# Who makes the low halves of the expert weights, and where the first chunk's rows lie: one Trainium2 core, a mixture of experts around an attention-like layer

## Chip, cores, metric

The kernel runs on one core of a Trainium2 chip. The metric is the device time of one execution in microseconds (us), median of the runs; lower is better. Engines: PE is TensorE's matmul, PEld its weight load, DVE is VectorE, ACT is ScalarE, POOL is GpSimd, SP is SyncE, which issues most DMAs.

## The reference, cut to what matters

```python
x = x + 0.5 * ffn(layernorm(x), ...)      # T = 2048 rows of D = 512
x = x + attn(layernorm(x), ...)           # 6 heads, a rotating recurrence over the rows
x = x + 0.5 * ffn(layernorm(x), ...)      # the same weights again

def ffn(x):                               # E = 8 experts, top 2, hidden 352
    scores = xf @ gate_w.T + gate_b + bias
    top_scores, top_idx = top_k(scores, 2)
    gates = softmax(top_scores)
    h = silu(einsum('td,ehd->teh', xf, w1) + b1)
    y = einsum('teh,edh->ted', h, w2) + b2
    out = einsum('ted,te->td', y, comb)   # comb: the gates at the chosen experts
```

## The kernel before, in words

Matrix products run in float16 with operands in two halves: a high half (the value times 256 for weights, rounded to float16) and a low half (what the rounding left). Three products (high by high, high by low, low by high) stand for one product of float32.

**Three phases.** The first mixture of experts (phase 0), the attention layer in four chunks of 512 rows, the second mixture (phase 1). A mixture first routes: `route` on VectorE and TensorE turns the scores into 39 slot tiles (`SLOT_TILES`) of 128 rows, each belonging to one expert, in the order of the experts. Its matmuls on TensorE are `route` (lines 647 to 654) and `slot_gates` (656 to 660). Then `slots` works tile by tile. GpSimd gathers a tile's 128 rows (line 537). TensorE transposes them (`xt`, through line 609), multiplies by w1 (`up`, 12 matmuls through line 615), transposes the hidden rows (`ht`, line 687) and multiplies by w2 (`down`, 9 matmuls through line 615). ScalarE makes the high half of the rows (`x_high`, line 972), the SiLU (line 977) and the high half of the hidden rows (`h_high`, line 982). VectorE makes the low halves (`x_low`, line 1361, and `h_low`, line 1372), adds the bias (line 1367) and scales the output (`y_out`, line 1380), which GpSimd scatters to `y_rows` (line 541). Each engine has its own list of instructions; a step's order is written out by hand: on TensorE `ht(t)`, `up(t+1)`, `xt(t+2)`, `down(t)`, on ScalarE `h_high(t)`, `silu(t+1)`, `x_high(t+2)`, on VectorE `h_low(t)`, `add_bias(t+1)`, `x_low(t+2)`, `y_out(t)`. The first 8 tiles (2 x `PEELED`) are written out, the rest is a hardware loop.

**The experts' weights.** In phase 0 the weights come as float32 (2944 values per partition and expert, `FW`) through three staging buffers `wstage`. VectorE makes both halves of experts 0 and 1 ahead of the routing (`split_low`, lines 1256 and 1259). For experts 2 to 7 ScalarE makes the high half (`split_high`, line 941) and VectorE the low half (`split_low`, line 1259): for expert 2 before the first `add_bias`, for experts 3 to 7 after the steps of tiles 0 to 4. SP loads expert e into buffer e mod 3 when the low half of expert e-3 is made (semaphore `w_ready`, line 354). When all are made, SP stores them to `w_saved` for phase 1 and fetches the attention weights in pieces, one per two tiles of the loop.

**The start of the attention.** SP waits until the outputs of the last tile are made (line 403, `m_yo`), loads the 512 rows of chunk 0 from `x_in` into the buffer `xgrp` (`group_in`, line 407), waits until the last scatter has landed (line 379), and then loads both contributions per tile of rows from `y_rows` into `y_first`, in eight DMAs (line 433). VectorE adds them (`first_rows`, lines 1452 and 1453), then takes the statistics of the four tiles (line 1250) and the moments. SP stores the rows (`group_out`), and loads chunk 1 into the same buffer (`next_group_in`) when they are stored and normalised; its contributions are added by GpSimd's DMAs (line 547).

The lines that the change touches, beside these: 371 (SP waits for all low halves), 530 (constants), 678 (`up` waits for its expert's weights), 996 to 1002 and 1229 to 1231 on ScalarE, 1401 to 1410 on VectorE.

## Time and profile before

| | |
|---|---|
| median of 3 runs | 895.51 us (894.84 to 895.96) |
| the profiled execution | 895.87 us |
| its span, first to last instruction | 894.1 us |
| busy PE, PEld | 737.8 us (83%), 406.8 us (45%) |
| busy DVE, ACT, POOL | 622.1 us (70%), 348.1 us (39%), 236.3 us (26%) |
| mean granted TensorE clock | 0.922 of 2.4 GHz |
| chain of waits, shares of the span | PE 70%, DVE 15%, DMA 5%, issue 4%, ACT 3% |

The span is what the trace covers. A busy share says how long an engine had an instruction in it, not how fast it went. The chain follows back from the last instruction, at each step to what released it. "issue" in it is time in which the engine waited for nothing that the profile shows. The granted clock is 1.0 at 2.4 GHz and 0.5 at 1.2 GHz.

### The profile page before, as it was taken

The numbers are of one execution on the slowest core, as the hardware profiler recorded it, in microseconds if no ns is written. First come the engines' busy times: TensorE is split into PE (matmuls) and PEld (weight loads), VectorE is DVE, ScalarE is ACT, GpSimd is POOL, SyncE is SP. The second block draws the span as 40 slices with busy tenths as digits, with TensorE's granted clock in tenths as the row PEclk, the third lists the DMA queues.
The fourth block names the chain that finished last, engine by engine and source line by source line (L and its number), as shares of the span: only waits on it lengthen the run. The fifth ranks groups of instructions, "written<-read, shape, count | busy, mean of one in ns | idle before, by whom it ended". The sixth has DMA issues, their size and how long they took to land.

```text
span 894.1 us, 13749 instructions
## 1 busy us (share of the span) xinstructions
PE 737.8 (83%) x4128; PEld 406.8 (45%) x4129; DVE 622.1 (70%) x1009; ACT 348.1 (39%) x600; POOL 236.3 (26%) x222
## 2 busy tenths in 40 slices
PE   8527699999990898997999999999529999999910
PEld 5215455555550444443444444444316565656600
DVE  6886755566654269999989998995775555555545
ACT  5714333434320546445644654532703323333300
POOL 3115644444520101101211011021113434444300
PEclk9859999999995899899999999999859999999965
DMA  9936568865425430610441201363836733333269
GB/s 321 385 111 207 186 223 317 322 243 176 143 83 199 99 89 21 121 49 0 88 78 24 60 12 25 120 166 128 311 112 223 255 107 117 117 106 117 84 223 374
DMA packets 45305, 137.25 MB, mean 153 GB/s; under 512 B 5840, under 2 KB 5840, under 8 KB 41936
## 3 DMA queue, kind: packets, MB, share of 16 engines
q1 hardware_dynamic: 27888, 86.38, 26.8%
q0 software_dynamic: 17376, 50.34, 20.5%
q8 instruction: 23, 0.38, 0.2%
q14 instruction: 18, 0.15, 0.0%
HBM read 85.32 MB, written 51.38 MB: 153 GB/s over the span
## 4 chain that ended last, share of the span: by engine, by line
PE 70%; DVE 15%; DMA 5%; issue 4%; ACT 3%; SPq 1%; POOL 0%; DVEq 0%; POOLq 0%; ACTq 0%
PE bank L615 59%; PE bank L609 4%; PE bank L687 3%; DMA space<-y_rows 2%; PE bank L804 2%; DVE space L1469 1%; DVE space L1466 1%; DVE space L1259 1%; DVE bst L1250 1%; SPq L477 1%; DMA y_rows<-space,slot_dst 1%; DVE space L1316 1%; DMA space<-x_in 1%; DMA space<-xn_rows,slot_src 1%; PE bank L738 1%
## 5 line engine op out<-in xcount | busy, mean ns | idle before, releaser
L615 PE MATMUL bank<-space 128*128 (+3 forms) x2958 | 581.0, 349 | 44.5 <-DVE space L1320 25.6
L615 PEld LDWEIGHTS bank<-space 128*128 128x128 f16 (+1 forms) x2958 | 274.3, 99 | 296.2 <-issue 37.7
L541 POOL DMA_INDIRECT y_rows<-space,slot_dst x78 | 99.7, 1278 | 158.2 <-DVE space L1380 158.2
L1361 DVE TENSOR_TENSOR space<-bank,space 128x512 f16<-128x512 f32 x78 | 54.0, 692 | 84.8 <-issue 43.2
L537 POOL DMA_INDIRECT space<-xn_rows,slot_src x78 | 76.3, 978 | 130.4 <-PE bank L609 70.0
L977 ACT ACTIVATE space<-space 128x352 f32<-128x352 f32 x78 | 38.7, 496 | 177.3 <-DVE space L1367 174.8
L1367 DVE SCALAR_TENSOR_TENSOR space<-bank,space 128x352 f32<-128x352 f32 x78 | 40.9, 524 | 64.0 <-PE bank L615 49.1
L609 PE MATMUL bank<-ident,space 128*128 128x128 f32 x440 | 67.6, 284 | 12.4 <-DMA space<-xn_rows,slot_src 10.5
L982 ACT ACTIVATE space<-bank 128x384 f16<-128x384 f32 x78 | 38.3, 491 | 77.9 <-PE bank L687 76.7
L1380 DVE TENSOR_SCALAR space<-bank,slot_gate 128x512 f32<-128x512 f32 x78 | 58.5, 750 | 12.9 <-PE bank L615 10.3
L1466 DVE SCALAR_TENSOR_TENSOR space<-space,cang 128x512 f32<-128x512 f32 x84 | 63.0, 750 | 5.5 <-ACT space L1051 3.3
L609 PEld LDWEIGHTS bank<-ident,space 128*128 128x128 f32 x440 | 55.1, 147 | 21.3 <-issue 14.1
L565 POOL TENSOR_TENSOR space<-space,power 128x8 f32<-128x8 f32 x12 | 23.8, 1986 | 137.4 <-ACT space L1079 137.4
L972 ACT ACTIVATE space<-bank 128x512 f16<-128x512 f32 x78 | 45.2, 580 | 26.8 <-PE bank L609 26.8
L1051 ACT ACTIVATE space<-bank 128x512 f32<-128x512 f32 x48 | 28.6, 595 | 60.0 <-PE bank L615 59.5
L1372 DVE TENSOR_TENSOR space<-bank,space 128x384 f16<-128x384 f32 x78 | 43.2, 554 | 10.0 <-ACT space L982 6.7
L1469 DVE SCALAR_TENSOR_TENSOR space<-space,conv_sb 128x512 f32<-128x512 f32 x72 | 48.7, 747 | 0.0
L687 PE MATMUL bank<-ident,space 128*128 128x128 f32 x234 | 40.4, 282 | 7.3 <-issue 7.0
L687 PEld LDWEIGHTS bank<-ident,space 128*128 128x128 f32 x234 | 27.0, 141 | 31.8 <-issue 25.0
L738 PE MATMUL bank<-ident,space 128*128 128x128 f32 x64 | 12.7, 344 | 32.8 <-ACT space L1020 30.5
L575 POOL DMA_DIRECT2D x_rows<-space x12 | 10.6, 882 | 101.2 <-ACT space L1100 101.2
L615 PE MATMUL bank<-space,gw 128*8 128x256 f32 x128 | 31.0, 386 | 0.6 <-ACT space L964 0.6
(172 smaller groups left out, 697.4 us busy)
## 6 DMA issues: line engine op xcount, KB each, us to landing
space<-ffn_w SPq DMA_DIRECT2D x8, 1472.0 KB, 10.0
w_saved<-space SPq DMA_DIRECT2D x8, 1472.0 KB
space<-w_saved SPq DMA_DIRECT2D x8, 1472.0 KB, 9.5
space<-y_rows SPq DMA_DIRECT2D x40, 256.0 KB, 6.0
xn_rows<-space SPq DMA_DIRECT2D x8, 1024.0 KB, 6.1
space<-x_in SPq DMA_DIRECT2D x7, 1024.0 KB, 5.3
space<-att_w SPq DMA_DIRECT2D x12, 518.0 KB
space<-y_rows POOLq DMA_DIRECT2D x6, 1024.0 KB, 9.3
```

Of the source, the lines that this page charges most:

```text
L537: gp.indirect_dma_start(dst, None, rows, bass.IndirectOffsetOnAxis(ap=index, axis=0)).then_inc(done, 16)
L541: gp.indirect_dma_start(y_rows, bass.IndirectOffsetOnAxis(ap=slot_dst[:, t:t + 1], axis=0), yo[:, t % 2], None).then_inc(y_st[t % 2], 16)
L609: last = pe.transpose(dst[:, k * P:(k + 1) * P], src[:, k * P:(k + 1) * P], ident[:, :])
L615: last = pe.matmul(dst, a, b, start=(n == 0), stop=(n == len(terms) - 1))
L687: last = pe.transpose(bank[4 + par][:, c * P:(c + 1) * P], hact[:, par, c * P:(c + 1) * P], ident[:, :])
L972: act.activation(xh[:, par], bank[par][:, :], ACT.Copy).then_inc(m_xh, 1)
L1361: v.tensor_tensor(xl[:, par], bank[par][:, :], xh[:, par], ALU.subtract).then_inc(m_xl, 1)
L1367: v.scalar_tensor_tensor(z[:, par], bank[2 + par][:, 0:HID], UNSCALE, b1_bc[:, bass.ds(ev * HID, HID)], ALU.mult, ALU.add).then_inc(m_zb, 1)
L1372: v.tensor_tensor(hl[:, par].rearrange("p a b -> p (a b)"), bank[4 + par][:, 0:KH * P], hh[:, par].rearrange("p a b -> p (a b)"), ALU.subt ...
L1380: v.tensor_scalar(yo[:, par], bank[6 + par][:, :], UNSCALE / GSCALE, slot_gate[:, bass.ds(t, 1)], ALU.mult, ALU.mult).then_inc(m_yo, 1)
L1466: seq(v.scalar_tensor_tensor(a, raw[:, p, kind, j:j + CH], cang[:, p, kind, j:j + 1], a, ALU.mult, ALU.add))
L1469: return ch(v.scalar_tensor_tensor(vcon[:, par, eo], raw[:, p, 2 + eo, j:j + CH], conv_sb[:, p, 2 + eo, j:j + 1], vcon[:, par, eo], ALU.mu ...
```

## The change

For experts 2, 3 and 4 the low half is no longer made by VectorE. TensorE multiplies the staged float32 weights by the identity, takes the high half times 1/256 away in the same bank of PSUM (a float16 product with a diagonal of -1/256, `unscale`), and ScalarE copies the difference times 256 to the low half. This goes in pieces of up to 512 columns (`CUTS`, six per expert), through four banks for experts 2 and 3 and two for expert 4. On TensorE the twelve pieces of experts 2 and 3 stand between the two counting products of `route` and the product over the one-hot rows; four pieces of expert 4 stand ahead of `xt(0)` and two behind it. On ScalarE the high half of expert 4 stands behind the twelve pieces of experts 2 and 3. VectorE keeps experts 5, 6, 7, after the steps of tiles 1, 2, 3; ScalarE's high halves of these come after tiles 0, 1, 2. SP waits for the new semaphore `w_low` for the buffers of experts 2 to 4. In the 8 written-out tiles of phase 0, ScalarE makes `x_high(t+2)` ahead of `silu(t+1)`.

Chunk 0's rows get a buffer of their own, so SP no longer waits for the last tile's outputs before it loads them, and chunk 1's rows are loaded right behind the `y_first` loads. These are four DMAs in place of eight. VectorE takes each tile's statistics right behind its sums. ScalarE's first write to the second `oh` buffer waits until chunk 0 is stored.

```diff
+BYPE = 3
+CUTS = [(at, min(CH, FW - at)) for at in range(0, FW, CH)]
+LOW_BANKS = (6, 7, 0, 1)
...
+        group_rows = [Layout(first_at)([TPC, D])] + [xgrp] * (NCH - 1)
...
             def weights_in(e):
-                if e >= STAGES:
+                if OWN <= e - STAGES < OWN + BYPE:
+                    sp.wait_ge(w_low, len(CUTS) * (e - STAGES - OWN + 1))
+                elif e >= STAGES:
                     sp.wait_ge(w_ready, e - STAGES + 1)
...
                 sp.wait_ge(s_slotg, 1)
-                sp.wait_ge(w_ready, E)
+                sp.wait_ge(w_ready, E - BYPE)
+                sp.wait_ge(w_low, len(CUTS) * BYPE)
...
             slot_weights()
-            sp.wait_ge(m_yo, SLOT_TILES + 2)
...
             def next_group_in(c):
-                sp.wait_ge(x1_st, 16 * c)
-                sp.wait_ge(c_xn, TPC * c)
+                if c > 1:
+                    sp.wait_ge(x1_st, 16 * c)
+                    sp.wait_ge(c_xn, TPC * c)
                 group_in(c)
...
             for i in range(TPC):
-                for k in (0, 1):
-                    sp.dma_start(y_first[:, k, i], y_rows[bass.ds(k * T + i * P, P), :]).then_inc(yf_in[i], 16)
+                sp.dma_start(y_first[:, :, i], y_rows[0:2 * T, :].rearrange("(k n p) d -> n p k d", k=2, p=P)[i]).then_inc(yf_in[i], 16)
+            next_group_in(1)
             group_out(0)
-            next_group_in(1)
...
+            def low_piece(e, i):
+
+                n = len(CUTS) * (e - OWN) + i
+                at, w = CUTS[i]
+                b = LOW_BANKS[n % 4] if e < OWN + BYPE - 1 else LOW_BANKS[n % 2]
+                pe.wait_ge(w_hi, e - OWN + 1)
+                if n >= 4:
+                    pe.wait_ge(w_low, n - (3 if e < OWN + BYPE - 1 else 1))
+                pe.matmul(bank[b][:, 0:w], ident[:, :], wstage[:, e % STAGES, at:at + w], start=True, stop=False, skip_group_check=True)
+                pe.matmul(bank[b][:, 0:w], unscale[:, :], wexp[:, e, at:at + w], start=False, stop=True,
+                          skip_group_check=True).then_inc(w_diff, 1)
...
                 products(bank[4][:, 0:NT * E], [(ones[:, :], chosen)]).then_inc(s_count, 1)
+                if not ph:
+                    pe.wait_ge(consts, 3)
+                    for e in range(OWN, OWN + BYPE - 1):
+                        for i in range(len(CUTS)):
+                            low_piece(e, i)
                 pe.wait_ge(s_ohs, ph + 1)
...
+                if not ph:
+                    for i in range(4):
+                        low_piece(OWN + BYPE - 1, i)
                 pe.wait_ge(s_route, ph + 1)
                 xt(0, 0, 0)
+                if not ph:
+                    for i in range(4, len(CUTS)):
+                        low_piece(OWN + BYPE - 1, i)
                 pe.wait_ge(m_xl, o + 2)
...
+            def low_piece(e, i):
...
+                act.wait_ge(w_diff, n + 1)
+                act.activation(wexp[:, e, FW + at:FW + at + w], bank[b][:, 0:w], ACT.Copy, scale=WSCALE).then_inc(w_low, 1)
...
+                def first_step(t, par):
+                    h_high(t, par)
+                    x_high(t + 2, par)
+                    silu(t + 1, 1 - par)
...
-                    step(t, t % 2)
-                    if not ph and 1 <= t <= 3:
-                        split_high(t + 4)
+                    if ph:
+                        step(t, t % 2)
+                    else:
+                        first_step(t, t % 2)
+                    if not ph and t < E - OWN - BYPE:
+                        split_high(OWN + BYPE + t)
...
-            for e in range(OWN + 1, 5):
-                split_high(e)
+            split_high(OWN + 1)
+            for e in (OWN, OWN + 1):
+                for i in range(len(CUTS)):
+                    low_piece(e, i)
+            split_high(OWN + 2)
+            for i in range(4):
+                low_piece(OWN + 2, i)
...
                 x_low(0, 0)
-                if not ph:
-                    split_low(OWN)
                 add_bias(0, 0)
...
-                    if not ph and OWN + 1 + t < E:
-                        split_low(OWN + 1 + t)
+                    if not ph and 1 <= t <= 3:
+                        split_low(OWN + BYPE + t - 1)
...
                 for i in range(TPC):
-                    v.wait_ge(yf_in[i], 32)
-                    seq(v.tensor_tensor(xgrp[:, i], xgrp[:, i], y_first[:, 0, i], ALU.add))
-                    v.tensor_tensor(xgrp[:, i], xgrp[:, i], y_first[:, 1, i], ALU.add).then_inc(c_sum, 1)
+                    v.wait_ge(yf_in[i], 16)
+                    seq(v.tensor_tensor(group_rows[0][:, i], group_rows[0][:, i], y_first[:, 0, i], ALU.add))
+                    v.tensor_tensor(group_rows[0][:, i], group_rows[0][:, i], y_first[:, 1, i], ALU.add).then_inc(c_sum, 1)
                     v.wait_ge(c_sum, i + 1)
+                    ch(v.bn_stats(bst[:, i], group_rows[0][:, i]))
+                ch.wait()
...
                 first_rows()
-                variance(xgrp)
+                moments()
```

## Rows read from the trace of the kernel before

**Rows 1.** Chain of waits, routing and tiles 0 to 5 (start us, us, what).

```profile
57.15 3.48 DMA space<-xn_rows,slot_src
...
80.36 2.13 PE bank L615 x9
```

**Rows 2.** Timeline of PE, 20 to 72 us (start us, us, operation).

```profile
28.47 1.89 PE L615 MATMUL bank<-space,gw 128*8 128x256 f32 x8
...
40.74 0.63 PE L615 MATMUL bank<-space,ones 128*128 128x128 f32 x2
54.16 1.25 PE L615 MATMUL bank<-space 128*128 128x39 f16 x32 [12.78 <-DVE space L1320]
60.76 1.09 PE L609 MATMUL bank<-ident,space 128*128 128x128 f32 x4 [5.36 <-DMA space<-xn_rows,slot_src]
63.57 3.70 PE L615 MATMUL bank<-space 128*128 x12 [1.72 <-DVE space L1361]
...
71.11 0.55 PE L687 MATMUL bank<-ident,space 128*128 128x128 f32 x3 [0.97 <-issue]
```

**Rows 3.** Timeline of PE in chunk 0 of the attention.

```profile
315.80 9.45 PE L615 MATMUL bank<-space 128*128 128x512 f16 x43
```

**Rows 4.** Timeline of ACT, routing and tiles 0 and 1.

```profile
39.15 2.64 ACT L941 ACTIVATE space<-space 128x2944 f16<-128x2944 f32 x1
...
74.56 0.58 ACT L972 ACTIVATE space<-bank 128x512 f16<-128x512 f32 x1
76.19 0.49 ACT L982 ACTIVATE space<-bank 128x384 f16<-128x384 f32 x1 [1.05 <-PE bank L687]
```

**Rows 5.** Stretches: us, busy PE, PEld, DVE, ACT, POOL, PEclk, DMA share, GB/s.

```profile
42.00:60.00 18.00, 1.25 (x32) 1.13 (x32) 16.71 (x43) 2.66 (x1) 2.16 (x2) 0.50 0.45 173
69.00:70.00 1.00, 1.00 (x38) 0.93 (x35) 0.69 (x1) 0.00 (x0) 0.34 (x1) 0.94 0.96 400
296.00:298.00 2.00, 0.96 (x4) 0.29 (x4) 0.00 (x0) 1.84 (x4) 0.00 (x0) 0.95 0.83 313
301.00:301.50 0.50, 0.50 (x4) 0.13 (x2) 0.00 (x0) 0.00 (x0) 0.38 (x1) 0.78 0.00 0
```

**Rows 6.** Timeline of DVE, tiles 0 to 7.

```profile
72.29 0.56 DVE L1372 TENSOR_TENSOR space<-bank,space 128x384 f16<-128x384 f32 x1 [1.91 <-ACT space L982]
...
76.53 3.22 DVE L1259 SCALAR_TENSOR_TENSOR space<-space 128x2944 f16<-128x2944 f32 x1
79.67 0.55 DVE L1372 TENSOR_TENSOR space<-bank,space 128x384 f16<-128x384 f32 x1
...
99.61 0.55 DVE L1372 TENSOR_TENSOR space<-bank,space 128x384 f16<-128x384 f32 x1
...
106.27 0.55 DVE L1372 TENSOR_TENSOR space<-bank,space 128x384 f16<-128x384 f32 x1
...
111.24 0.56 DVE L1372 TENSOR_TENSOR space<-bank,space 128x384 f16<-128x384 f32 x1 [1.38 <-ACT space L982]
...
115.98 0.55 DVE L1372 TENSOR_TENSOR space<-bank,space 128x384 f16<-128x384 f32 x1
```

**Rows 7.** Chain of waits, the last scatter of each phase and the rows behind.

```profile
268.53 6.27 DMA y_rows<-space,slot_dst
...
285.07 2.48 DVE bst L1250 x4
...
855.62 2.73 DMA y_rows<-space,slot_dst
```

**Rows 8.** Timeline of DVE, the first rows of the attention.

```profile
278.22 0.69 DVE L1452 TENSOR_TENSOR space<-space 128x512 f32<-128x512 f32 x1 [2.98 <-DMA space<-y_rows]
...
280.71 0.69 DVE L1452 TENSOR_TENSOR space<-space 128x512 f32<-128x512 f32 x1 [1.08 <-DMA space<-y_rows]
```

**Rows 9.** Timeline of SP, end of phase 0.

```profile
268.28 0.40 SPq L407 DMA_DIRECT2D space<-x_in  x1
274.82 3.68 SPq L433 DMA_DIRECT2D space<-y_rows  x8
```

More of the change, by code:

```diff
@@ L113, in build @@
         minus = sb("minus", [P, P], F16)
+        unscale = sb("unscale", [P, P], F16)
         sel = sb("sel", [44, 2, PAIRS, P], F16)
@@ L250, in build @@
         on = lay([2, CH])
+        first_at = lay.at
         oh.append(lay([2 * PAIRS, CH], F16))
@@ L283, in build @@
         w_ready = sem("w_ready")
+        w_diff = sem("w_diff")
+        w_low = sem("w_low")
         w_save = sem("w_save")
@@ L402, in _ @@
             slot_weights()
-            sp.wait_ge(m_yo, SLOT_TILES + 2)
             def group_in(c):
-                sp.dma_start(xgrp, rows4(x_in, c)).then_inc(cg_in, 16)
+                sp.dma_start(group_rows[c], rows4(x_in, c)).then_inc(cg_in, 16)
             def group_out(c):
@@ L413, in group_out @@
                     sp.wait_ge(cy_in[1], 16 * c)
-                sp.dma_start(rows4(x_rows, c), xgrp).then_inc(x1_st, 16)
+                sp.dma_start(rows4(x_rows, c), group_rows[c]).then_inc(x1_st, 16)
             def next_group_in(c):
-                sp.wait_ge(x1_st, 16 * c)
-                sp.wait_ge(c_xn, TPC * c)
+                if c > 1:
+                    sp.wait_ge(x1_st, 16 * c)
+                    sp.wait_ge(c_xn, TPC * c)
                 group_in(c)
@@ L530, in more_constants @@
                     select(sel_rows, sel_rows, ALU.not_equal, 1.0, -first, [[-1, NAB], [0, 64]], 1)
+                seq(gp.memset(unscale[:, :], 0.0))
+                seq(gp.affine_select(out=unscale[:, :], in_=unscale[:, :], compare_op=ALU.not_equal, fill=-UNSCALE, base=0,
+                                     pattern=[[-1, P]], channel_multiplier=1))
                 seq(gp.memset(minus[:, :], 0.0))
@@ L676, in up @@
                             pe.wait_ge(w_back[t], 16)
+                        elif OWN <= t < OWN + BYPE:
+                            pe.wait_ge(w_low, len(CUTS) * (t - OWN + 1))
                         else:
-                            pe.wait_ge(w_ready, t + 1)
+                            pe.wait_ge(w_ready, t + 1 if t < OWN else t + 1 - BYPE)
                     pe.wait_ge(m_xl, o + t + 3)
@@ L941, in split_high @@
                 act.activation(wexp[:, e, 0:FW], wstage[:, e % STAGES], ACT.Copy, scale=WSCALE).then_inc(w_hi, 1)
+            def low_piece(e, i):
+                n = len(CUTS) * (e - OWN) + i
+                at, w = CUTS[i]
+                b = LOW_BANKS[n % 4] if e < OWN + BYPE - 1 else LOW_BANKS[n % 2]
+                act.wait_ge(w_diff, n + 1)
+                act.activation(wexp[:, e, FW + at:FW + at + w], bank[b][:, 0:w], ACT.Copy, scale=WSCALE).then_inc(w_low, 1)
             def normalise_row(ph, n):
@@ L991, in step @@
                     x_high(t + 2, par)
+                def first_step(t, par):
+                    h_high(t, par)
+                    x_high(t + 2, par)
+                    silu(t + 1, 1 - par)
                 x_high(0, 0)
+                if not ph:
+                    for i in range(4, len(CUTS)):
+                        low_piece(OWN + BYPE - 1, i)
                 silu(0, 0)
@@ L996, in slots @@
                 for t in range(2 * PEELED):
-                    step(t, t % 2)
-                    if not ph and 1 <= t <= 3:
-                        split_high(t + 4)
+                    if ph:
[4 more added lines that the diff above has]
+                        split_high(OWN + BYPE + t)
                 split = PEELED if ph else PEELED + PIECES
                 if not ph:
-                    act.wait_ge(w_ready, E)
+                    act.wait_ge(w_ready, E - BYPE)
+                    act.wait_ge(w_low, len(CUTS) * BYPE)
                     with act.Fori(PEELED, split) as j:
@@ L1019, in normalise @@
                     act.wait_ge(c_xt, TPC * c + i - 1)
-                act.activation(xnt[:, i % 2], xgrp[:, i], ACT.Identity, scale=rstd[:, 0, 0, i:i + 1],
+                act.activation(xnt[:, i % 2], group_rows[c][:, i], ACT.Identity, scale=rstd[:, 0, 0, i:i + 1],
                                bias=rstd[:, 0, 1, i:i + 1]).then_inc(c_xn, 1)
@@ L1092, in gate_high @@
                     act.wait_ge(c_out, TPC * (c - 1))
+                if u == PAIRS:
+                    act.wait_ge(x1_st, 16)
                 act.activation(oh[c % 2][:, 2 * p:2 * p + 2], on, ACT.Copy).then_inc(c_oh, 1)
```

## The prediction

> **What bounds the kernel now.** I read the page's slices first, then the chain of waits, then the timelines of the two stretches that the diff touches, then SP's queue. The chain lies on TensorE for 70% of the span, but not where the change is. From 42 to 60 us, while VectorE turns scores into slots, TensorE is busy 1.25 us of 18, at the granted clock 0.50 (1.2 GHz), and VectorE 16.71 [rows 5]. In the first tiles VectorE decides: one low half takes 3.22 us, and `h_low` of the next tile starts only behind it [rows 6]. `h_low` starts at 72.29 for tile 0 and 79.67 for tile 1 (7.38 apart), at 99.61 for tile 4 and 106.27 for tile 5 (6.66), at 111.24 and 115.98 for tiles 6 and 7 (4.74, no split between) [rows 6]. The third place is the change of phase: the last scatter of phase 0 takes 6.27 us from issue to landing, that of phase 1 takes 2.73 [rows 7]. SP issues the load of chunk 0 at 268.28 and the scatter starts at 268.53 [rows 7, 9].
>
> The profiled execution took 895.87 us, its span is 894.1, so 1.77 lie around it; the median of the runs is 895.51, 0.36 below it. I work out the change of the span and take it from the median. About 0.2% (1.8 us) is what a measurement of this kernel can tell from no change.
>
> **Price of a piece.** On TensorE a piece is a float32 product of 512 columns and a float16 product of 512. Four float32 products of 256 columns took 1.89 us at full clock [rows 2], so one of 512 costs 2 x 0.47 = 0.945. 43 float16 products of 512 took 9.45 [rows 3], 0.22 each. A piece is 1.16 us at 2.4 GHz and twice that, 2.3, at 1.2 GHz. That has not run here in this mixture, so the bounds are 0.58, since ScalarE empties a bank of 512 in that time [rows 4], and 2.3. I take 1.16, because both terms come from the same kinds of product. The sixth piece has 384 columns, so six count as 5.75. ScalarE's 0.58 per piece hides behind TensorE's.
>
> **Routing.** The pieces of experts 2 and 3 begin when the counting products end, 41.4 [rows 2]. Expert 3's high half is ready at 41.8 [rows 4], in time. The clock is at 0.50. It rose about 5.5 us after dense matmuls began at 63.57 (0.94 in the mean from 69 to 70), and 3.4 us after a fall at 297.8 (the stretch from 296 has 0.95, so 0.2 us at half; that from 301.0 has 0.78, so it rose at 301.2) [rows 2, 5]. I take a rise at 45.2: 3.8 us at half give 1.65 pieces, the other 9.85 (twelve count 11.5) take 11.4 us, end 56.6. The one-hot product that started at 54.16 is 2.4 us late; it took 1.25 at half clock [rows 2], some 0.7 now, so it ends 57.3 and not 55.4. That is on the path: the first gather's index comes 1.9 us late. The gather took 3.48 us to land [rows 1], so it lands about 62.6.
>
> ScalarE empties the last piece at 57.2, makes expert 4's high half (2.64 [rows 4]) until 59.9, and TensorE makes four pieces until 64.6 (4 x 1.16). Only then comes `xt(0)`, which started at 60.76 [rows 2]; the gather is in by then, so its lateness is covered. `xt(0)` 0.55 at full clock, two pieces 2.03, `up(0)` from 67.2, 1.8 in place of 3.70 at half clock [rows 2], `xt(1)` 0.45, the 64 gate products 1.7 (38 of them took 1.00 [rows 5]), the 0.97 idle ahead of `ht(0)` as before: `ht(0)` at 72.1 and not at 71.11 [rows 2]. **Cost +1.0.** Expert 2's low half of 3.22 us that VectorE loses ahead of the first `add_bias` gave nothing: TensorE was in `up(0)` until 67.27.
>
> **The first tiles.** Between tiles 0 and 1 VectorE has no split any more, 4.74 in place of 7.38. But ScalarE now makes expert 5's high half behind `silu(1)`: 2.64 us from about 75.1 on the old scale, so `h_high(1)`, which started at 76.19 [rows 4], starts near 77.75, 1.5 late, and nothing hides that. The step takes 6.0 to 6.2: **-1.4**, bounded by 0 (the high half takes all of it) and -2.64. The steps of tiles 1, 2, 3 keep their split. Moving `x_high` ahead of the SiLU I cost at nothing: in a split step `y_out` waits for `down`, which starts 0.14 behind the end of `h_low` and takes 2.13 [rows 1], so an earlier `x_low` only waits longer; elsewhere `down` covers the SiLU that comes 0.6 later. Tile 4 loses its split: 6.66 becomes 4.7, **-1.95**. The buffers of experts 5, 6, 7 come free earlier than before, so no load is late. The longer list of constants on GpSimd lies in an idle stretch before the first gather; if that cover were gone it would be under 1 us.
>
> **Start of the attention.** Chunk 0's load no longer runs beside the last scatter. I take the landing of phase 1's last scatter, 2.73 in place of 6.27: **-3.54**, bounded by 0. By the Trainium skill ("DMA: Bandwidth & Descriptors", Queues, rings and completion order) each DMA engine goes round-robin between the queues that have work, a packet at a time. By this rule the scatter would lose to the load only about its own transfer time, some 1 us, and the sum below would come to 891.0. The trace shows 3.54 between the two landings, and I follow it. Of the `y_first` loads, eight issues took 3.68 us [rows 9]; tile 0 now needs one of four and not two of eight, **-0.4**. VectorE began tile 0 at 278.22 and idled 1.08 before tile 1 [rows 8]; its statistics, 0.62 of the 2.48 [rows 7], now fill that hole, **-0.7**. Bounds for both together: 0, if chunk 1's load behind them slows the last tiles, and -2.5. The moves on SP and GpSimd for chunk 1 only fill an earlier buffer; VectorE is busy with chunk 0 long after. If that cover were gone, chunk 1 would only be ready earlier.
>
> **Sum.** +1.0 - 1.4 - 1.95 - 3.54 - 0.4 - 0.7 = -7.0; 895.5 - 7.0 = 888.5 us.
>
> **Rivals.**
> - *The clock falls once more.* TensorE idles from 57.3 to 59.9. At 297.8 it fell though TensorE had been busy 0.96 us of the 2 around it [rows 5]. Against it: the gap is one of 2.6 us between stretches of dense matmuls, where that stretch was thin throughout. If it falls, expert 4's pieces start at 2.3 each for some 3.4 us (half that is lost, 1.7) and the rest shifts, up to `up(0)` at its old 3.70: +3, 891.5. Chance 0.2.
> - *The scatter is not slow because of the load.* Sharing by turns costs it only about 1 us; the other 2.5 stay: 891.0. That is the time the skill's rule gives. For it: the late landing may be the writes' own. Against it: the same instruction with nothing beside it took 2.73 [rows 7]. Chance 0.12.
> - *The first gather collides.* Expert 6's load is issued when expert 3's low half is done, about 57.3, right ahead of the gather. If that costs what it cost the scatter, 3.54, the rows land at 66.1, 1.5 behind the pieces: 890.0. Chance 0.1.
> - *Slower.* TensorE stays at 1.2 GHz through the pieces. Its place is between `s_count` and `s_ohs`: 41.4 + 11.5 x 2.3 = 67.9, 11.3 late; expert 4's six add 6.7 more, `up(0)` 1.9: +20, 908. It outweighs the gain as soon as the pieces lose 7 us more than planned, at 1.8 us each for the 11.5. For it: 0.50 through this whole stretch [rows 5]; pairs of float32 loads may not hide either (a counting product of 128 columns took 0.63 at half clock [rows 2], four times that is 2.5 for a float32 product alone). Against it: nothing makes TensorE wait between pieces, and such stretches raised the clock. Chance 0.06.
> - *It does not do what it says:* ScalarE's high half eats the whole of the step between tiles 0 and 1, and the statistics move nothing: 890.5 to 891. Inside the range.
>
> **How the numbers follow.** The forecast has 0.45, the rivals 0.2, 0.12, 0.1, 0.06, the rest 0.07 (half of it better than forecast: a rise of the clock at once and both holes filled give about 886). All but the slower one and a heap of several end below 893.7, so faster 0.87, same 0.06, slower 0.07. The range runs from 885.5 to 893: below, the bounds of the small terms together (-2.5 for 1.1 and no loss in the routing would be -9.4); above, the clock's second fall with a gather that collides.
>
> **What would show it.** Right: low pieces of about 1.16 us on TensorE between 42 and 57, the clock at 1.00 by 47, `xt(0)` near 64.6; `h_low` of tile 1 near 79.3 and of tile 5 near 103.9; a last scatter of under 3.5 us; the statistics in four single rows between the sums; the second tile's sums of the attention about 6.5 us earlier than 280.71 and the span 887. Wrong: pieces of 2 us or more, a wait of VectorE for `s_inv` over 5 us, a last scatter that still takes 6 us with no load beside it, or a chain that shows DMA waits where chunk 1 loads.

## The result, and the profile after

The changed kernel takes 888.14 us (median of 6 runs, 885.63 to 891.24), the kernel before 895.81 in the same set (6 runs, 894.84 to 896.36). The ratio is 0.992, 95% interval 0.9901 to 0.9939: faster by 0.6 to 1.0%. The forecast was 888.5. Two later sets of the same changed kernel gave 3.9 and 6.4 us less than before; all 24 runs have a median of 889.57, and the mean of the three differences is 6.0 us (5.4 when each set counts by its number of runs), not 7.7. The profiled execution took 889.80 us, span 888.0.

The page of the changed kernel, part 1 (busy us, share of the span, instructions) and the slices of the granted clock (tenths of 2.4 GHz):

```profile
PE 756.9 (85%) x4182; PEld 414.6 (47%) x4183; DVE 612.3 (69%) x1006; ACT 358.5 (40%) x618; POOL 232.0 (26%) x224
...
PEclk9899999999995998998999999999759999999975
```

TensorE has 19 us more work and VectorE 10 less, as three low halves of 3.2 us changed hands. The mean clock rose from 0.922 to 0.934.

**The routing.** Timeline of PE in the changed kernel (start us, us, operation):

```profile
39.82 0.77 PE L627 MATMUL bank<-space,before 128*128 128x128 f32 x2 [6.55 <-DVE space L1357]
...
42.94 1.46 PE L667 MATMUL bank<-space,ident 128*128 128x512 f32 x2
...
45.53 1.02 PE L667 MATMUL bank<-space,ident 128*128 128x512 f32 x2
46.38 0.38 PE L668 MATMUL bank<-space,unscale 128*128 128x512 f16 x1
46.60 1.02 PE L667 MATMUL bank<-space,ident 128*128 128x512 f32 x2
...
54.66 0.97 PE L627 MATMUL bank<-space 128*128 128x39 f16 x32
57.95 2.07 PE L667 MATMUL bank<-space,ident 128*128 128x512 f32 x2 [2.32 <-ACT space L978]
...
63.78 0.60 PE L621 MATMUL bank<-ident,space 128*128 128x128 f32 x4
```

A piece takes 1.07 us (45.53 to 46.60). The twelve pieces end at 54.7, and the first 3 us of them ran at a granted clock of 0.50. The one-hot product starts at 54.66 (54.16 before [rows 2]). Then TensorE waits 2.32 us for ScalarE's high half of expert 4, and the first piece behind it takes 2.07 us for its float32 product where 1.02 is usual: the clock was down again. Stretches of the changed kernel (us, busy PE, PEld, DVE, ACT, POOL, PEclk, DMA share, GB/s):

```profile
57.00:58.00 1.00, 0.05 (x1) 0.05 (x1) 0.86 (x7) 0.90 (x1) 0.62 (x1) 0.73 0.91 318
58.00:61.00 3.00, 3.00 (x5) 1.27 (x6) 2.97 (x5) 0.52 (x1) 1.53 (x2) 0.52 0.97 405
```

**The first tiles.** For the steps the start of `y_out` is the better scale than that of `h_low`, since `y_out` waits for `down`, the last thing that TensorE does in a step. Timeline of DVE, changed kernel, tiles 0, 1, 2, 4 and 5 (L1443 is `y_out`, L1322 the split):

```profile
76.36 0.75 DVE L1443 TENSOR_SCALAR space<-bank,slot_gate 128x512 f32<-128x512 f32 x1 [0.63 <-PE bank L627]
...
81.21 0.75 DVE L1443 TENSOR_SCALAR space<-bank,slot_gate 128x512 f32<-128x512 f32 x1 [0.90 <-PE bank L627]
81.87 3.21 DVE L1322 SCALAR_TENSOR_TENSOR space<-space 128x2944 f16<-128x2944 f32 x1
...
87.86 0.75 DVE L1443 TENSOR_SCALAR space<-bank,slot_gate 128x512 f32<-128x512 f32 x1 [1.28 <-PE bank L627]
...
101.17 0.75 DVE L1443 TENSOR_SCALAR space<-bank,slot_gate 128x512 f32<-128x512 f32 x1 [1.28 <-PE bank L627]
...
105.71 0.75 DVE L1443 TENSOR_SCALAR space<-bank,slot_gate 128x512 f32<-128x512 f32 x1 [0.68 <-PE bank L627]
```

The same rows of the kernel before:

```profile
75.86 0.75 DVE L1380 TENSOR_SCALAR space<-bank,slot_gate 128x512 f32<-128x512 f32 x1
...
82.51 0.75 DVE L1380 TENSOR_SCALAR space<-bank,slot_gate 128x512 f32<-128x512 f32 x1
...
102.47 0.75 DVE L1380 TENSOR_SCALAR space<-bank,slot_gate 128x512 f32<-128x512 f32 x1
...
109.11 0.75 DVE L1380 TENSOR_SCALAR space<-bank,slot_gate 128x512 f32<-128x512 f32 x1
```

Tile 0 is 0.50 later than before. Both profiles count from their own first instruction; counted from the counting products (39.82, and 40.18 before) it is 36.54 us against 35.68, 0.86 later. The profile of attention_only, whose code up to there is that of the kernel before, has 34.39, so this figure moves by over 1 us between profiles of the same code. The lengths of the steps do not (6.64 to 6.66 in both). Between tiles 0 and 1 are 4.85 us (6.65 before), between 4 and 5 4.54 (6.64). A step that keeps its split takes 6.65 in both. At tile 8 the changed kernel is 3.9 us ahead (120.81 against 124.69), at the last output 3.6 (263.93 against 267.50).

**The start of the attention.** Chain of waits of the changed kernel:

```profile
264.96 2.72 DMA y_rows<-space,slot_dst
267.69 0.02 issue
267.70 3.54 DMA space<-y_rows
...
271.37 0.70 DVE space L1513
272.09 0.70 DVE space L1514
272.79 0.02 issue
272.82 0.69 DVE bst L1516
273.51 0.60 DVE space L1513
```

The last scatter lands in 2.72 us (6.27 before [rows 7]). Sums and statistics run without a hole from 271.37 to 279.64, 8.27 us; before they took 9.32 from 278.22 [rows 8] to 287.54. So the statistics end 7.9 us earlier. From there 1.8 us are given back: 6.1 is the difference of the spans. The first 0.75 go in the transposes ahead of the dense products, which begin 11.1 us after the statistics (290.74 - 279.64), and 10.35 before. The dense products then win 0.5 back. Timeline of PE, changed kernel:

```profile
290.74 16.90 PE L627 MATMUL bank<-space 128*12 128x512 f16 x72 [0.69 <-ACT space L1086]
```

and the kernel before:

```profile
297.89 17.44 PE L615 MATMUL bank<-space 128*12 128x512 f16 x72 [0.69 <-ACT space L1030]
```

The lead is 7.7 us at their end and still 7.72 where the second chunk's dense products begin. In them it falls to 6.3. Chain of waits of the changed kernel, and its stretch (columns as above):

```profile
418.64 5.96 PE bank L627 x18
```

```profile
418.00:423.00 5.00, 5.00 (x15) 2.07 (x15) 4.86 (x8) 2.31 (x3) 0.00 (x0) 0.53 0.61 189
```

The same of the kernel before:

```profile
426.36 4.53 PE bank L615 x18
```

```profile
421.00:426.00 5.00, 2.96 (x12) 2.19 (x13) 4.90 (x8) 4.48 (x8) 0.00 (x0) 0.50 0.00 0
426.00:431.00 5.00, 5.00 (x22) 2.13 (x20) 4.86 (x7) 2.12 (x4) 0.00 (x0) 0.85 0.62 205
```

Eighteen matmuls take 1.43 us more. Both kernels have the clock down here, but in the changed one the half clock lies over the dense products, and in the one before mostly ahead of them (0.50 in 421 to 426), where TensorE is busy 2.96 of 5 us and the chain of waits lies mostly on ScalarE. In the second mixture, whose first `up` takes 3.70 us in place of 3.30, the lead sinks to 5.65 (`up(1)`: 668.72 against 674.37), and 0.45 of it comes back by the end. So what is given back is, for the most part, where the clock stands in this run. From the second chunk on the profile of attention_only keeps its lead of 6.1 to the end of the attention, and fill_only its 7.1. In the first chunk both win 1.6 us more (72 products in 15.81 us in place of 17.44): their clock stood at 1.00 there, and in the kernel before at 0.50 from 297.8 to 301.2.

### The profile page after: what moved, and what is told of

The parts are those of the page before. It is cut to its first block, busy times and chain, and to the rows that moved or that the text cites. A ratio compares the mean times of both kernels' runs of the same rounds, so it can differ in the third digit from the quotient of the medians.

```text
span 888.0 us, 13883 instructions
## 1 busy us (share of the span) xinstructions
PE 756.9 (85%) x4182; PEld 414.6 (47%) x4183; DVE 612.3 (69%) x1006; ACT 358.5 (40%) x618; POOL 232.0 (26%) x224
## 4 chain that ended last, share of the span: by engine, by line
PE 72%; DVE 15%; DMA 4%; issue 4%; ACT 3%; SPq 1%; POOL 0%; DVEq 0%; POOLq 0%; ACTq 0%
PE bank L627 58%; PE bank L621 4%; PE bank L718 3%; DMA space<-y_rows 2%; PE bank L667 2%; DVE space L1529 2%; PE bank L841 2%; DVE space L1532 1%; DVE space L1322 1%; DVE bst L1313 1%; DMA space<-x_in 1%; PE bank L775 1%; DMA y_rows<-space,slot_dst 1%; DVE space L1710 1%; DVE space L1709 1%
## 5 line engine op out<-in xcount | busy, mean ns | idle before, releaser
L553 POOL DMA_INDIRECT y_rows<-space,slot_dst x78 | 94.0, 1205 | 159.0 <-DVE space L1443 159.0
L1443 DVE TENSOR_SCALAR space<-bank,slot_gate 128x512 f32<-128x512 f32 x78 | 58.5, 750 | 19.4 <-PE bank L627 17.4
```

The source lines that it names most:

```text
L553: gp.indirect_dma_start(y_rows, bass.IndirectOffsetOnAxis(ap=slot_dst[:, t:t + 1], axis=0), yo[:, t % 2], None).then_inc(y_st[t % 2], 16)
L1443: v.tensor_scalar(yo[:, par], bank[6 + par][:, :], UNSCALE / GSCALE, slot_gate[:, bass.ds(t, 1)], ALU.mult, ALU.mult).then_inc(m_yo, 1)
```

## The experiments

Each run is compared with runs of the kernel before on the same chip. Their medians were 894.68 (35 runs; the first four experiments), 895.33 (17; the next four) and 893.55 (24; the last four). Single runs of one kernel spread over 3 to 8 us, so the small questions are decided in the timelines, by the length of a stage. Where a difference in us and a ratio do not quite agree: the first is that of the medians, the second weighs all runs.

**attention_only.** The kernel before with the buffer `group_rows`, SP's order, four `y_first` DMAs and the statistics between the sums.

```diff
-            sp.wait_ge(m_yo, SLOT_TILES + 2)
...
+        group_rows = [Layout(first_at)([TPC, D])] + [xgrp] * (NCH - 1)
...
-                variance(xgrp)
+                moments()
```

> The kernel before with the second half of the change alone: chunk 0's rows in their own buffer and loaded early, chunk 1's load ahead, four y_first DMAs, statistics between the sums. My theory: -3.5 us from the last scatter, -1.1 from the sums and statistics, about -4.6, so 891.2 us, last scatter under 3.5 us. Rival (DMA engines only take turns, the scatter loses about 1 us to the load): -2.1, 893.7 us, last scatter still above 5 us.

Measured: 889.28 us, ratio 0.9953 (0.9935 to 0.997), 5.4 us less than before. The scatter landed in 2.71 us, sums and statistics took 8.28. The ratio makes it 4.2 us; the forecast of 4.6 for this half lies between the two and inside the interval (2.7 to 5.8 us).

**weights_only.** The changed kernel with that half undone.

```diff
+            sp.wait_ge(m_yo, SLOT_TILES + 2)
...
-        group_rows = [Layout(first_at)([TPC, D])] + [xgrp] * (NCH - 1)
...
-                moments()
+                variance(xgrp)
```

> The change with its second half undone: only the low halves of three experts moved and the order on ScalarE in the first eight tiles. My prediction's terms: +1.0 -1.4 -1.95 = -2.35, so 893.4 us. The trace of the changed kernel has the last output of phase 0 3.6 us earlier than before; if that is what the part is worth alone, 892.2 us. Rival (what is won in the first tiles is lost later, so the parts do not add up): 895 us or more.

Measured: 892.65 us, ratio 0.9973 (0.9956 to 0.9991), 2.0 less by the medians and 2.4 by the ratio, near the -2.35 of the prediction. The scatter is back at 5.96 us. The two halves add up to -7.4 by the medians and -6.6 by the ratios, where the whole has -3.9 and -4.8 in the same set (below) and -7.7 and -7.2 in the first. Within this noise nothing shows that they do not add up. In this profile one split step took 8.33 us in place of 6.66, which had not been expected.

**load_late.** The changed kernel, one wait put back.

```diff
             slot_weights()
+            sp.wait_ge(m_yo, SLOT_TILES + 2)
```

> The changed kernel with one wait put back: SP waits for the last tile's outputs before it loads chunk 0's rows, so the 1 MB load again runs beside the last scatter. Collision theory: +3.5 us, scatter about 6.3 us from issue to landing. Turn-taking alone: +1.0 us, scatter 3.7. If the change of the scatter had nothing to do with the load: +0, scatter 2.7.

Chain of waits of this run:

```profile
262.74 5.66 DMA y_rows<-space,slot_dst
268.42 3.46 DMA space<-y_rows
```

The scatter beside the load takes 5.66 us, 2.9 more than in every run without it (2.71 to 2.73 in eleven profiles). For the scatter the collision theory stands; taking turns alone was to cost about 1. The +3.5 us of it are not seen in the time: 891.14 against 890.81 of the changed kernel in the same set, 0.3 us more by the medians and 1.8 by the ratios, with intervals of about 3 us from end to end. In this profile 2.5 us go between the last output and the first sum (10.3 against 7.8), and 2.8 came from elsewhere, as the next run shows.

**changed_again.** The changed kernel unchanged, beside the three above.

> The changed kernel unchanged. Its six runs so far fall into two heaps, 885.6 to 886.5 and 889.8 to 891.2. If the heaps come from when TensorE's granted clock falls and rises, a profile from the lower heap has fewer or shorter stretches at 0.50 than the profiled run at 889.8 (which has 3.4 us at half clock from 57.5 and 30.7 us between the attention and the second mixture). If they do not, the stretches at 0.50 are the same in both and the difference lies in DMA landings.

Measured: 890.81 us (12 runs, 885.6 to 892.59), ratio 0.9946 (0.9928 to 0.9965). No profile of the lower heap came out of it (this one is at 891.68), so the heaps were not compared as planned. The 24 runs of all three sets lie between 885.60 and 892.59 with no gap wider than 1.2 us. But it can be laid beside load_late, whose code up to the last tile is the same. Timeline of PE behind the one-hot product, changed_again:

```profile
58.79 1.94 PE L667 MATMUL bank<-space,ident 128*128 128x512 f32 x2 [2.32 <-ACT space L978]
60.53 0.63 PE L668 MATMUL bank<-space,unscale 128*128 128x512 f16 x1
```

and load_late:

```profile
57.06 1.12 PE L668 MATMUL bank<-space,ident 128*128 128x512 f32 x2 [2.32 <-ACT space L979]
58.02 0.38 PE L669 MATMUL bank<-space,unscale 128*128 128x512 f16 x1
```

The gap is the same, 2.32 us. In changed_again the clock fell at its end (about 59.0, by 0.74 from 58 to 60), in load_late it did not. From the counting products to the first `y_out` it is 36.91 us in changed_again and 34.06 in load_late: 2.85 us. Of these 0.98 lie ahead of the gap, where the clock rose earlier in load_late (its one-hot product starts 14.51 us behind the counting products, 15.49 in changed_again). From the first piece behind the gap to the first `y_out` it is 18.13 against 16.26, so the fall cost 1.9 us. Then changed_again pays once more in a split step, where TensorE waits 1.98 us for VectorE ahead of `down`:

```profile
92.91 3.80 PE L627 MATMUL bank<-space 128*128 x9 [1.98 <-DVE space L1435]
```

```profile
88.00:92.00 4.00, 2.94 (x21) 2.04 (x19) 3.58 (x2) 2.60 (x3) 2.55 (x1) 1.00 0.25 72
92.00:96.00 4.00, 3.09 (x8) 1.26 (x9) 1.80 (x4) 0.50 (x1) 2.13 (x2) 0.64 0.36 123
```

Nine matmuls take 3.80 us, not 2.11, and that step is 8.33 us long.

**warm_gap.** Eleven products that nobody reads fill the gap (added work, the output is the same).

```diff
+                    for i in range(WARM):
+                        pe.matmul(bank[3][:, :], unscale[:, :], wexp[:, 0, 0:CH], start=True, stop=True, skip_group_check=True)
                     for i in range(4):
                         low_piece(OWN + BYPE - 1, i)
```

> The changed kernel with eleven float16 products of 512 columns, whose result nobody reads, between the one-hot product and expert 4's first piece, where TensorE waits 2.3 to 2.6 us for ScalarE's high half. In three of four profiles of kernels with the pieces the granted clock was 0.50 for 3.4 us from about 57, and the first piece began with 2.07 us in place of 1.02. Theory (that fall lengthens the way to the first tile): no stretch at 0.50 there, expert 4's four pieces in 4.3 us, h_low of tile 0 about 1.7 us earlier counted from the counting products, time -1.2 us in the mean, since not every run has the fall. Rival (the fall has nothing to do with the gap, or the gather decides anyway): nothing, or up to +0.5 from the added products.

Measured: 888.56 us, ratio 0.9922 (0.9897 to 0.9947), 6.8 less than before. No clock fall behind the one-hot product. The first `y_out` came 35.39 us after the counting products; the six profiles of kernels with the same order up to there and a fall in the gap have 36.5 to 37.0. A part of this is when the clock first rose. From the first piece behind the gap it is 17.06 us here and 17.96 to 18.51 in the six, so the gap's fall costs 0.9 to 1.45 us more than filling it (load_late, with neither, has 16.26). One profile without a fall does not show that the added products prevent it, since two of the eight with the gap unfilled have none there either. And a split step then took 8.01 us with the clock down, and the time is not told apart from the changed kernel's.

**high5_early.** ScalarE's high half of expert 5 ahead of the first SiLU.

```diff
+                    split_high(OWN + BYPE)
                 silu(0, 0)
...
-                    if not ph and t < E - OWN - BYPE:
+                    if not ph and 1 <= t < E - OWN - BYPE:
```

> The changed kernel with ScalarE's high half of expert 5 moved from behind tile 0's step to behind the last piece of expert 4, ahead of the first SiLU, where ScalarE idles 2.1 us. Prediction's term: between tiles 0 and 1 that high half is exposed, 5.57 us from h_low to h_low where 4.6 would do, so -1.0 us. Rival (the step has other reasons, as the 1.2 us of issue ahead of h_low): the interval stays at 5.5.

Measured: 889.82 us, ratio 0.9926 (0.9898 to 0.9954). From `y_out(0)` to `y_out(1)` 4.50 us in place of 4.85. The exposed part was 0.35 us, not 1.0 to 1.5. Moved ahead of the first SiLU the high half is exposed there: `ht(0)` starts 7.74 us behind `xt(0)`, and 7.11 in load_late, where the clock was up as well. So this profile shows no gain on balance (its clock fell besides in `up(1)`, which took 3.49 us in place of 1.95). The reason for the 0.35 stands in the changed kernel's timelines of ACT and PE, the high half, `h_high(1)` behind it, and `down(1)`:

```profile
75.29 2.65 ACT L978 ACTIVATE space<-space 128x2944 f16<-128x2944 f32 x1
77.84 0.48 ACT L1026 ACTIVATE space<-bank 128x384 f16<-128x384 f32 x1
```

```profile
76.48 1.95 PE L627 MATMUL bank<-space 128*128 x12
78.27 0.60 PE L621 MATMUL bank<-ident,space 128*128 128x128 f32 x4
79.05 2.11 PE L627 MATMUL bank<-space 128*128 x9 [0.18 <-DVE space L1435]
```

`h_high(1)` is late, but what needs it is `down(1)`, and TensorE has `up(2)` and `xt(3)` to do before that. It waited 0.18 us.

**silu_first.** The old order on ScalarE in the first eight tiles.

```diff
                 def first_step(t, par):
                     h_high(t, par)
-                    x_high(t + 2, par)
                     silu(t + 1, 1 - par)
+                    x_high(t + 2, par)
```

> The changed kernel with ScalarE's old order, SiLU ahead of x_high, in the first eight tiles of phase 0. The prediction costed the order at nothing: all intervals of h_low within 0.1 us of the changed kernel's, time the same. Rival: the interval from tile 4 to tile 5 is 3.70 us in the changed kernel's profile and 4.7 was forecast; if the order gives that, it goes back to 4.7 here, +1.0 us.

Measured: 889.55 us, ratio 0.9941 (0.9919 to 0.9963). By `y_out`: the step between tiles 0 and 1 takes 5.25 us in place of 4.85, the three split steps 6.65, 6.65, 6.66 as before, tiles 4 to 5 4.58 (4.54). So the order is worth 0.4 us in one step, where it lets ScalarE's high half start earlier, and nothing in the others. The rival falls: between the `h_low` of tiles 4 and 5 there are 3.71 us here, as in the changed kernel, so the 3.70 was no matter of the order.

**two_experts.** VectorE keeps expert 4 too.

```diff
-BYPE = 3
+BYPE = 2
...
-                    if not ph and t < E - OWN - BYPE:
-                        split_high(OWN + BYPE + t)
+                    if not ph and 1 <= t <= 3:
+                        split_high(t + 4)
...
-                    if not ph and 1 <= t <= 3:
-                        split_low(OWN + BYPE + t - 1)
+                    if not ph and t <= 3:
+                        split_low(OWN + BYPE + t)
```

> The changed kernel with experts 2 and 3 alone made by TensorE and ScalarE; VectorE keeps 4 to 7, behind tiles 0 to 3. Theory (the third expert costs its pieces ahead of xt(0) and saves a split): xt(0) near 60.9 in place of 63.8, at half clock again, h_low of tile 0 about 1.5 us earlier, the interval of tiles 0 to 1 near 7.2 in place of 5.6, so -1.5 + 1.7, the same time within 0.5. Rival (the third expert's pieces are the larger cost): 1.5 us faster.

Measured: 894.72 us, ratio 0.9991 (0.9972 to 1.001). Both theories fall: this is 0.6 us less than before, where the changed kernel had 3.9 to 7.7 less. `xt(0)` started at 61.83, but it waited for the gather, which took 4.89 us to land (3.48 before [rows 1]) beside the weight loads that the pieces had made early. The clock was down for 10.2 us behind the one-hot product, since no pieces fill that stretch. And two of the split steps took 7.2 us, because VectorE now waited for a high half. Timeline of DVE, two_experts:

```profile
92.20 3.23 DVE L1313 SCALAR_TENSOR_TENSOR space<-space 128x2944 f16<-128x2944 f32 x1 [0.48 <-ACT space L974]
```

In the new order ScalarE makes the SiLU behind the wait for `add_bias`, and the high half of the same step only behind that. The changed kernel makes each high half one step ahead and has no such wait. So this run tests two things at once, the number of experts and the later high halves (0.6 us in each of two steps). Its step between tiles 0 and 1 was 8.14 us where 7.2 was expected, with the clock down in `down(1)` (3.61 us for nine matmuls in place of 2.11). How many experts are best with the high halves one step ahead stays open.

**high4_early.** Expert 4's high half ahead of the last four pieces of expert 3.

```diff
                 for i in range(len(CUTS)):
                     low_piece(e, i)
-            split_high(OWN + 2)
+                    if e == OWN + 1 and i == 1:
+                        split_high(OWN + 2)
```

> The changed kernel with ScalarE's high half of expert 4 moved ahead of the last four pieces of expert 3: four banks let TensorE run on meanwhile. TensorE then has no gap behind the one-hot product. Theory (the gap of 2.3 to 3 us, and the fall of the clock behind it, lie on the path to the first tile, the gather does not): expert 4's first piece within 0.3 us of the one-hot product's end, xt(0) at 21 to 22 us after the counting products in place of 24 to 25, the first y_out 2 to 3 us earlier by the same scale, time -2 us. Rival (the first gather decides, which landed 4.9 us from its issue where it was waited for): xt(0) waits for the gather and the gain is under 1.5 us.

Timeline of PE of this run:

```profile
54.00 0.97 PE L627 MATMUL bank<-space 128*128 128x39 f16 x32
54.92 1.10 PE L667 MATMUL bank<-space,ident 128*128 128x512 f32 x2
...
62.11 0.63 PE L621 MATMUL bank<-ident,space 128*128 128x128 f32 x4 [2.65 <-DMA space<-xn_rows,slot_src]
```

The gap behind the one-hot product is gone, as meant, and comes back as a gap of 2.65 us ahead of `xt(0)`. The gather was issued at 56.73 and took 5.25 us. 889.25 us, ratio 0.9935 (0.9912 to 0.9958): the rival was right, a hidden wait took the place of the one removed. The clock fell right behind the new gap (0.50 for 3.4 us from 63.2). The first `y_out` came 36.20 us behind the counting products, 36.54 in the changed kernel.

**fill_only.** Eight products that nobody reads ahead of `down` in the steps of tiles 1 to 3 (added work).

```diff
+                    if not ph and isinstance(t, int) and 1 <= t <= 3:
+                        pe.wait_ge(m_yo, o + t + 1)
+                        for i in range(8):
+                            pe.matmul(bank[6 + par][:, :], unscale[:, :], wexp[:, 0, 0:CH], start=True, stop=True, skip_group_check=True)
                     pe.wait_ge(m_hl, o + t + 3)
```

> The changed kernel with eight float16 products that nobody reads ahead of down in the steps of tiles 1 to 3, where TensorE waits about 2 us for VectorE's split. Four of six profiles with moved low halves show one of these steps at 7.5 to 8.3 us in place of 6.65 and the granted clock at 0.50 for 3.4 us in it. Theory (idle of 2 us in 6.65 lets the clock fall, by chance of where it lies): all these steps at 6.65 and no stretch at 0.50 between 70 and 100 us; time -1 us in the mean. Rival (the fall is not tied to the idle): a step over 7.5 us again.

Measured: 891.14 us, ratio 0.9974 (0.9963 to 0.9985), not better than the changed kernel. The steps of tiles 2 to 4 took 6.65, 6.65, 6.66 with the clock up, and so did those of both_fill (below). Without the added products one split step is longer in six of ten profiles of kernels with moved low halves (7.55 to 8.33), so two without a fall agree with the theory and do not show it. I put the products one tile too early: VectorE's split behind tile 1 holds up `down` of tile 2. In the step of tile 1 they met no wait and stood in the way (timeline of PE):

```profile
78.84 1.89 PE L725 MATMUL bank<-space,unscale 128*128 128x512 f16 x8
80.56 2.11 PE L627 MATMUL bank<-space 128*128 x9
```

That step took 6.23 us in place of 4.85, and the steps between tiles 5 and 8 lost 0.8 more: the whole sequence now lies later against the transfers in the background (DMA share 1.05 from 108 to 112 us), and `y_out(6)` waited for a scatter to land, which it does not in the changed kernel. Timeline of DVE:

```profile
114.39 0.75 DVE L1447 TENSOR_SCALAR space<-bank,slot_gate 128x512 f32<-128x512 f32 x1 [1.68 <-DMA y_rows<-space,slot_dst]
```

**both_fill.** high4_early, high5_early and fill_only together.

```diff
+                    split_high(OWN + BYPE)
                 silu(0, 0)
...
+                        for i in range(8):
+                            pe.matmul(bank[6 + par][:, :], unscale[:, :], wexp[:, 0, 0:CH], start=True, stop=True, skip_group_check=True)
```

> The version that the runs so far point to: expert 4's high half early, expert 5's high half ahead of the first SiLU, and the filling products of fill_only. If the parts add up: -2 -0.4 -1 against the changed kernel, 885 to 887 us. Rival (the first gather holds xt(0), as in two_experts): about -1.5, 888.

Measured: 890.80 us, ratio 0.9965 (0.9948 to 0.9981). The clock stayed up from 45 to 270 us, and it is still no faster than the changed kernel: `xt(0)` waited for the gather again (5.26 us), the products misplaced by a tile cost 1.4, and then the attention began 5.6 us before the clock rose. Its 72 products took 18.50 us, where the profiles range from 15.81 (attention_only, silu_first, fill_only) to that. None of the versions beats the changed kernel beyond its interval.

**changed_third.** The changed kernel unchanged, beside the last three.

> The changed kernel unchanged, on the same chip as the three above, since its medians were 888.1 and 890.8 in two sets. By the clock theory every run draws how many falls it has in the gap behind the one-hot product (1.7 us each) and in the split steps (0.9 to 1.7 us): between 886 and 892, median near 889.5. If the two sets differ by the chip and not by the draw, this one is tight.

Measured: 887.20 us (6 runs, 885.99 to 889.65), ratio 0.9932 (0.991 to 0.9953), 6.4 less than before. It is tighter than the second set (3.7 us over 6 runs, 7.0 over 12) and lower than the median forecast here. Its profile shows a fall in the gap and a split step of 8.33 us, so the draw is there too. That the clock makes most of the spread stands in the runs themselves: over all 24 runs of the changed kernel the mean granted clock goes from 0.930 (891.26 to 892.59 us, four runs) to 0.939 (885.63), the correlation with the time is -0.85, and 0.001 more clock goes with 0.76 us less. Whether the chip has a part in the difference of the sets stays open.

## Why the prediction was right, point by point

- **Price of a piece**, 1.16 us: measured 1.07. The float32 product takes 0.86, not 0.945 as scaled from a row of 256 columns; why that row cost more per column no run shows.
- **Rise of the clock**, forecast at 45.2: 43.8, which is 4.0 us after the counting products began at 39.82. This was one draw: in the twelve profiles with the pieces it is 2.9 to 5.5 us. So the twelve pieces ended at 54.7, not 56.6, and the one-hot product came 0.9 us behind VectorE's last row and not 2.4.
- **Gap and clock behind it.** The forecast had the gap (2.6 us, measured 2.32) and took the clock to stay up; the fall was a rival at 0.2. It happened in the profiled run and in five of the seven other profiles with this gap. Its chance was too low, and its price too high (3 us; 1.9 by changed_again against load_late). The pieces' lower price paid for it: `xt(0)` at 63.78 where 64.6 was forecast, `ht(0)` at 71.61 where 72.1 was. The cost of the routing was +0.5 by these two profiles, not +1.0. That this term came out near is in part luck: counted from the counting products the cost is +0.86, it is over 2 us against the profile of attention_only, and load_late, whose clock rose earlier and did not fall, is 1.6 us faster to the first `y_out` than the kernel before.
- **Tiles 0 to 1**, -1.4 with ScalarE's high half exposed by 1.5: measured -1.80, and exposed is only 0.35 (high5_early). This step of the argument failed. I measured it from `h_low` to `h_low`, and forgot that TensorE works on `up(2)` and `xt(3)` before it needs what is late.
- **The new order on ScalarE**, costed at 0: 0.4 us in one step, nothing in split steps (silu_first).
- **Tile 4**, -1.95: -2.10. Another 0.5 us came in the steps behind it, up to tile 8.
- **The scatter**, -3.54: -3.55 (6.27 to 2.72), and load_late puts 2.9 of it back with one wait. The rule of the Trainium skill ("DMA: Bandwidth & Descriptors", Queues, rings and completion order) that I had set against it tells how the engines share; by it as I applied it the loss is about one transfer time, 1 us, and these runs show three times that.
- **Sums and statistics**, -1.1: -0.79. The single DMA per tile gave nothing: 3.68 us from the scatter's landing to the first sum, 3.42 before. This step of the argument failed too: counting fewer issues ahead of the first sum, as the forecast did for its 0.4, does not tell when the first transfer lands. The statistics in the holes gave 1.05.
- **The first gather collides**, a rival at 0.1: right in itself. It lands in 4.9 to 5.3 us where it is waited for, 1.4 to 1.8 more than before. In the changed kernel the pieces cover it, by an estimate with about 1 us to spare (issued at 57.38, and 5.25 later is 62.6, where `xt(0)` starts at 63.78). Where the clock stays up this is gone: in load_late and high5_early `xt(0)` starts 4.98 and 5.24 us behind the gather's issue. So without the fall the gather would decide next, as in high4_early.
- **Slower, and not doing what it says:** neither; the clock rose 3.0 us after the first piece began.
- **The signs.** `h_low` of tile 1 came at 78.35 (79.3 forecast) and of tile 5 at 102.01 (103.9), the second tile's sums at 273.43, 7.3 us earlier and not 6.5, the span is 888.0 (887). The stages to there did better than forecast, and what lies behind them took it back.

The terms measured give +0.5 -1.8 -2.1 -0.5 -3.55 -0.8 = -8.3, the stages up to the end of the statistics -7.9 (the phase's loop loses 0.3). The forecast of -7.0 came near the profiled pair's -6.1 because the gains in the first tiles were forecast too small, and what comes behind was not in the sum at all: 1.8 us given back in the profiled run, most of it in the second chunk's first products, as the clock stood at half there. The mechanism was right in its main terms (the scatter, the two steps without a split). That 888.5 lies 0.4 us from the 888.14 of the first set is luck: the three sets give 3.9 to 7.7 us.

## What to carry to other kernels

Measure a stage at the point that waits last for it, here `y_out` behind `down`, and ask of anything late what the consumer has to do before it needs it. Work moved onto an idle TensorE can also raise the clock for what follows (`up(0)` took 1.96 us in place of 3.70), but only as long as no gap opens behind it: the fall behind the gap of 2.32 us took back 1.9. A removed gap can reappear at the next late thing, here a gather slowed by loads that the same change had made earlier. A load that nobody awaits yet should be issued before a latency-bound small DMA at the end of a phase, not beside it.

## What the runs showed of the hardware that was not expected

- A small indirect DMA loses more beside a bulk load than the time of its own transfer (an estimate: 0.7 us for 256 KB at the 400 GB/s of [rows 5]): the last scatter (256 KB) takes 2.71 to 2.73 us alone and 5.66 to 6.27 beside 1 MB; the first gather 3.48 alone and 4.89 to 5.26 beside a weight load.
- The same program with the same gap of 2.32 us finds the granted clock at 1.00 in one run and at 0.50 in another. A fall lasted about 3.4 us. In the gap it cost 1.9 us (changed_again against load_late), and a split step of 6.65 became 7.55 to 8.33. The kernel before has the same waits of about 2 us in its five split steps, and neither its profile nor that of attention_only shows a fall in them.
- A float32 product of 512 columns followed by a float16 product of 512 into the same bank takes 0.86 + 0.22 us at a granted clock of 1.00 and 2.1 to 2.3 in all at 0.50, with the next piece right behind.
- While VectorE makes a low half (two operands in SBUF, 3.21 us), GpSimd's issue of a scatter takes 3.7 us in place of 1.0; the kernel before has the same beside its splits (3.72 to 3.74). This is the timeline of POOL in the changed kernel, without and with a split beside it:

```profile
77.39 1.01 POOL L553 DMA_INDIRECT y_rows<-space,slot_dst  x1 [1.80 <-DVE space L1443]
...
82.24 3.71 POOL L553 DMA_INDIRECT y_rows<-space,slot_dst  x1 [2.11 <-DVE space L1443]
```
